# Stacked loads over two DMA queues, weight loads moved, and unread products in TensorE's waits, in a one-core decoder layer

## What is computed

```python
q, k = l2norm(q), l2norm(k)                       # self-attention
attn = softmax(einsum('bhnd,bhkd->bhnk', q/sqrt(D), k/sqrt(D)) / temperature)
x = layernorm(x + proj(attn @ v) + proj_b)
Srel = skew(einsum('bhsd,ld->bhsl', q, Er))       # cross-attention
attn = softmax(where(causal, (q @ k.T + Srel) / sqrt(dh), -inf))
x = layernorm(x + attn @ v)
top1 = argmax(softmax(x @ router_w + router_b))   # experts
for i in range(8):
    a, g = split(x @ w1[i] + b1[i])
    out += where(top1 == i, (a * sigmoid(g)) @ w2[i] + b2[i], 0)
x = layernorm(x + out)
```

## Time and profile before

| | us |
|---|---|
| median of 3 runs | 289.67 (287.71 to 290.94) |
| profiled execution, whole | 290.45 |
| its span, first to last instruction | 288.7 |
| TensorE busy in it | 235.4 |
| VectorE busy | 202.0 |
| ScalarE busy | 140.7 |
| GpSimd busy | 91.8 |
| mean granted clock of TensorE | 0.915 |

### The profile page before, as it was taken

One profiled execution on the slowest core, in us unless ns is written; L12 is line 12 of the kernel. 1 busy time (PEld: TensorE's weight loads), 2 busy tenths in 40 slices (PEclk: granted clock), 3 DMA queues, 4 the chain that ended last, 5 costly groups with the idle time before them and its releaser, 6 DMA issues.

```text
span 288.7 us, 8043 instructions
## 1 busy us (share of the span) xinstructions
PE 235.4 (82%) x3170; PEld 173.4 (60%) x3171; DVE 202.0 (70%) x579; ACT 140.7 (49%) x326; POOL 91.8 (32%) x128
## 2 busy tenths in 40 slices
...
PEclk9959799955999988999799899999999689999995
...
GB/s 65 195 396 184 41 168 154 109 76 179 218 60 166 104 119 22 94 189 213 94 111 112 3 41 70 190 115 115 194 175 61 16 20 187 187 179 345 141 7 0
DMA packets 30036, 36.92 MB, mean 128 GB/s; under 512 B 6967, under 2 KB 23333, under 8 KB 29616
## 3 DMA queue, kind: packets, MB, share of 16 engines
...
q10 hardware_dynamic: 256, 0.03, 0.1%
HBM read 25.00 MB, written 11.80 MB: 127 GB/s over the span
## 4 chain that ended last, share of the span: by engine, by line
PE 33%; issue 20%; DVE 17%; POOL 10%; DMA 9%; ACT 7%; SPq 2%; POOLq 1%; DVEq 0%; ACTq 0%
DVE negm L1084 6%; POOL out L777 5%; PE SB L1529 4%; PE MA L1365 3%; DMA w_sb<-parts_a 3%; POOL rs L772 3%; PE SA L1409 3%; DMA shift_a<-nmT 2%; DMA parts_a<-SpA 2%; PE MB L1345 2%; PE SA L1424 2%; PE SB L1388 2%; PE MA L1435 2%; ACT P L851 2%; SPq L467 2%
## 5 line engine op out<-in xcount | busy, mean ns | idle before, releaser
L1084 DVE TENSOR_REDUCE negm<-SA 128x2 bf16<-128x512 f32 x64 | 41.2, 685 | 11.4 <-PE SA L1409 11.0
L851 ACT ACTIVATE P<-SA 128x512 f32<-128x512 f32 x64 | 35.7, 599 | 14.6 <-PE SA L1424 13.1
L1163 DVE TENSOR_REDUCE negm<-MB 128x4 bf16<-128x512 bf16 x32 | 22.0, 686 | 8.3 <-PE MB L1345 8.0
L735 POOL TENSOR_TENSOR rs<-ve,half 128x2 f32<-128x2 f32 (+1 forms) x9 | 6.1, 682 | 64.9 <-DVE ve L1045 64.9
L797 ACT ACTIVATE Sb<-SB 128x512 bf16<-128x512 f32 x22 | 13.1, 597 | 24.5 <-PE SB L1529 24.2
L889 ACT ACTIVATE P2b<-SB 128x1024 f32<-128x1024 f32 x14 | 14.1, 1023 | 8.9 <-PE SB L1548 8.8
L1409 PE MATMUL SA<-w_sb 96*128 96x256 bf16 x64 | 12.5, 297 | 6.7 <-DVE negm L1084 4.7
L1524 PE MATMUL SB<-QH,KZ 128*128 128x64 bf16 x320 | 16.9, 198 | 1.1 <-DMA QH<-parts_b 1.1
L1435 PE MATMUL MA<-P,V 128*32 128x256 f32 x256 | 17.3, 402 | 0.0
L1548 PE MATMUL SB<-identb,negm 128*128 128x128 bf16 x176 | 14.3, 219 | 3.0 <-issue 1.9
L777 POOL DMA_INDIRECT out<-P,token x15 | 15.3, 1019 | 3.8 <-issue 3.1
...
## 6 DMA issues: line engine op xcount, KB each, us to landing
...
```

The lines of the kernel that those rows point to most:

```text
L851: a.activation(P1[:, grp % 2, kt, 2 * i:2 * i + 2, :].rearrange("p h t -> p (h t)"), SA[:, bank_a("st", b, u), :], ACT.Exp).then_inc(s["ex ...
L1084: v.tensor_reduce(out=negm1[:, hp // 4, qt, :, hp % 4], in_=SA[:, bank_a("d", b, u), :].rearrange("p (g k) -> p g k", g=2), axis=AX.X, op= ...
L1163: v.tensor_reduce(out=negm2[:, qb, :], in_=MBb[:, 0:512].rearrange("p (c k) -> p c k", c=4), axis=AX.X, op=ALU.max, negate=True).then_inc( ...
```

## The change

It has three parts. First, of the four stacked loads of a stage the two of the high rows (QS and KS rows 48 to 95, Z/QZ and QH from row 64) are issued by GpSimd instead of SP, with semaphores of their own (qs_high, qz_high, qh_high). For stage A GpSimd does this at A1.qsin; for stage B at a new step A2.zin, which stands some steps behind A2.q2T in batches 0 and 1 and right behind it in 2 and 3. A1.qsin.1 moves ahead of A1.k0.1. GpSimd waits there for the same writes as SP does. Second, W.u3 moves from behind B.tr3.1 to behind A2.ln1.2, W.pk0 from behind A2.k2T.2 to behind A2.zin.2, and W.u4 from behind B.sh2.1 to behind B.sc1.2. Third, TensorE gets steps K.w, each with a number of unread products (`unread`), at 18 places from batch 0's first transposes to the second batch's weighing, 46 products, and 2 more between the two products of A1.qkv.1. In batch 0's steps they write to MB, in batch 1's to bank 3 of SB.

```diff
-    A1.qkv.0 A1.vcp.0 A1.k1.1 A1.qkn.0 W.bl0.0 W.bl1.0 W.bl2.0 W.bl3.0 A1.qkT.0 A1.k5.0 A1.k2.0 A1.qkv.1 A1.ex0.0
...
-    A2.st4.0 A2.st5.0 A1.k6.0 A1.k0.1 A2.st6.0 A2.st7.0 A1.qsin.1 A2.pv0.0 A2.pv1.0 A2.st8.0 A2.st9.0 A2.k2T.0
-    A2.st11.2 A2.st12.2 B.tr3.1 W.u3.0 A2.k2T.2 W.pk0.0 A2.st13.2 B.sh2.1 W.u4.0 A2.st14.2 B.sh3.1 A2.st15.2 B.tr4.1
...
+    A1.qkv.0 A1.vcp.0 A1.k1.1 A1.qkn.0 W.bl0.0 W.bl1.0 W.bl2.0 W.bl3.0 K.w4.0 A1.qkT.0 A1.k5.0 A1.k2.0 K.w3.0
+    A1.qkv.1 A1.ex0.0 A1.ex1.0 A1.d0.0 A1.d1.0 A1.ex2.0 A1.ex3.0 A2.cx.0 A1.d2.0 A1.d3.0 A2.xpb.0 K.w2.0 A1.d4.0
+    A1.ex7.0 A1.d12.0 A1.d13.0 W.v6.0 K.w1.0 A1.d14.0 A1.d15.0 K.w3.0 A1.shT1.0 A1.qkn.1 A1.k8.1 A2.st0.0 A1.k4.0
+    A2.st1.0 A1.qkT.1 A2.st2.0 A2.st3.0 K.w1.0 A2.st4.0 A2.st5.0 A1.k6.0 A1.qsin.1 A1.k0.1 A2.st6.0 A2.st7.0
+    A2.pv0.0 A2.pv1.0 A2.st8.0 A2.st9.0 K.w1.0 A2.k2T.0 A2.st10.0 A2.st11.0 K.w3.0 A2.nm0.0 A2.st12.0 A1.k3.1
+    A2.st13.0 K.w2.0 A2.st14.0 W.u0.0 A2.st15.0 A2.pv2.0 A2.pv3.0 A1.d0.1 A1.d1.1 K.w2.0 A1.d2.1 A1.d3.1 A2.nm1.0
+    A1.d4.1 A1.vcp.1 A1.d5.1 A2.oT.0 A1.d6.1 A2.proj.0 A1.d7.1 A2.ln1.0 B.v.0 A1.qkv.2 K.w3.1 A1.shT0.1 A1.shin0.1
+    K.w2.1 A2.x1T.0 A1.d8.1 A1.d9.1 K.w2.1 A1.d10.1 A1.d11.1 A2.q2T.0 A1.d12.1 A1.d13.1 K.w7.1 A1.d14.1 A1.d15.1
+    A1.qkn.2 A2.zin.0 K.w1.1 A2.st0.1 A2.st1.1 A1.shT1.1 K.w3.1 A1.qkT.2 A1.shin1.1 B.build.0 A2.st2.1 A2.st3.1
+    K.w1.1 A2.st4.1 A2.st5.1 A2.st6.1 A2.st7.1 B.rest.0 A2.pv0.1 A2.pv1.1 K.w5.1 A2.st8.1 A2.cx.1 B.sc0.0 A2.nm0.1
...
+    A1.d2.3 A2.proj.2 A2.ln1.2 W.u3.0 B.sc6.1 B.sh5.1 B.pv0.1 A1.d3.3 A1.d4.3 A2.x1T.2 B.nm0.1 A2.q2T.2 A2.zin.2
+    W.pk0.0 A1.d5.3 B.tr6.1 A1.d6.3 A1.vcp.3 B.sc7.1 A1.d7.3 B.tr7.1 A1.d8.3 B.sh6.1 A1.d9.3 B.sh7.1 A1.d10.3
+    B.sc0.2 B.sc1.2 W.u4.0 B.tr0.2 A2.st0.3 B.sc2.2 A2.st1.3 B.tr1.2 A2.st2.3 B.sc3.2 B.tr2.2 B.sh0.2 B.sh1.2
...
-PACED_BY = {("A1", "qsin"): ("qs_in", 64, 0, 0), ("A1", "d"): ("sa_full", 16, 1, 1), ("A1", "shT0"): ("m_in0", 16, 0, 16),
-            ("A1", "shT1"): ("m_in1", 16, 0, 16), ("A2", "st"): ("st_full", 16, 1, 1), ("A2", "q2T"): ("qz_in", 32, 0, 32),
+PACED_BY = {("A1", "qsin"): ("qs_in", 32, 0, 0), ("A1", "d"): ("sa_full", 16, 1, 1), ("A1", "shT0"): ("m_in0", 16, 0, 16),
+            ("A1", "shT1"): ("m_in1", 16, 0, 16), ("A2", "st"): ("st_full", 16, 1, 1), ("A2", "q2T"): ("qz_in", 16, 0, 16),
...
             def q_k_in(b):
...
-                for g in range(2):
-                    rows = slice(g * SR, (g + 1) * SR)
-                    load(QSs[b % 2][rows, :, :].rearrange("r (a g j) t -> r g a (j t)", g=2, a=2)[:, g, :, :],
-                         half_stack(parts_a, 0, g).rearrange("r (a j) t -> r a (j t)", a=2), "qs_in")
-                    load(KSs[b % 2][rows, :, :], half_stack(parts_a, 1, g), "qs_in")
+                load(*query_rows(b, 0), "qs_in")
+                load(*key_rows(b, 0), "qs_in")
...
             def cross_queries(b):
...
-                for half_ in (0, 64):
-                    load(Zs[b % 2][half_:half_ + SR, :, q], stack(parts_b, 0)[:, :, q], "qz_in")
+                load(*cross_rows(b, 0), "qz_in")
...
-                by_half(lambda at, heads: QHs[b % 2][at:at + SR, heads, q], parts_b, 0, q, "qh_in")
+                load(*cross_half(b, 0), "qh_in")
...
+            def high_stacks(b):
+                wait(pool, "st_full", (b - 1) * 16)
+                pool.wait_ge(s["pa_out"], b * 96)
+                for rows, parts in (query_rows(b, 1), key_rows(b, 1)):
+                    pool.dma_start(rows, parts).then_inc(s["qs_high"], 16)
+
+            def high_queries(b):
+                wait(pool, "sc_full", (b - 1) * NQB)
+                if b < 2:
+                    pool.wait_ge(s["z_fill" if b == 0 else "qz_fill"], 1)
+                    pool.wait_ge(s["kz_fill" if b == 0 else "qh_fill"], 1)
+                pool.wait_ge(s["pq_out"], b * 48 + 48)
+                for name, (rows, parts) in (("qz_high", cross_rows(b, 1)), ("qh_high", cross_half(b, 1))):
+                    pool.dma_start(rows, parts).then_inc(s[name], 16)
...
-            def stay_busy(n):
+            def stay_busy(n, room=SB[:, 3, :]):
                 for _ in range(n):
-                    mm(SB[:, 3, :], identb[:, :], identb[:, :].unsqueeze(1).broadcast_to([P, 4, P]), start=True, stop=True)
+                    mm(room, identb[:, :], identb[:, :].unsqueeze(1).broadcast_to([P, 4, P]), start=True, stop=True)
+            def unread(b, n):
+                stay_busy(n, MB[:, :] if b == 0 else SB[:, 3, :])
...
+                    elif b == 1 and i == 0:
+                        unread(0, 2)
```

More of the change, by code:

```diff
@@ L68 @@
-    A2.st10.0 A2.st11.0 A2.nm0.0 A2.st12.0 A1.k3.1 A2.st13.0 A2.st14.0 W.u0.0 A2.st15.0 A2.pv2.0 A2.pv3.0 A1.d0.1
-    A1.d1.1 A1.d2.1 A1.d3.1 A2.nm1.0 A1.d4.1 A1.vcp.1 A1.d5.1 A2.oT.0 A1.d6.1 A2.proj.0 A1.d7.1 A2.ln1.0 B.v.0
-    A1.qkv.2 A1.shT0.1 A1.shin0.1 A2.x1T.0 A1.d8.1 A1.d9.1 A1.d10.1 A1.d11.1 A2.q2T.0 A1.d12.1 A1.d13.1 A1.d14.1
-    A1.d15.1 A1.qkn.2 A2.st0.1 A2.st1.1 A1.shT1.1 A1.qkT.2 A1.shin1.1 B.build.0 A2.st2.1 A2.st3.1 A2.st4.1 A2.st5.1
-    A2.st6.1 A2.st7.1 B.rest.0 A2.pv0.1 A2.pv1.1 A2.st8.1 A2.cx.1 B.sc0.0 A2.nm0.1 A2.st9.1 A2.st10.1 B.tr0.0
@@ L73 @@
-    B.sc1.0 A2.st11.1 A2.st12.1 B.sc2.0 A1.qsin.2 B.tr1.0 A2.xpb.1 A2.st13.1 A2.st14.1 A2.k2T.1 A2.st15.1 B.sc3.0
-    B.tr2.0 B.sh0.0 A2.pv2.1 A2.pv3.1 B.sh1.0 A1.d0.2 B.tr3.0 A1.d1.2 W.u1.0 W.v7.0 A2.nm1.1 A1.d2.2 B.sc4.0 B.sh2.0
-    A2.oT.1 B.sh3.0 A1.d3.2 B.tr4.0 A2.proj.1 A2.ln1.1 B.sc5.0 B.pv0.0 A1.d4.2 A2.x1T.1 A1.d5.2 B.sh4.0 B.nm0.0
-    A2.q2T.1 A1.d6.2 A1.d7.2 B.tr5.0 A1.vcp.2 A1.qkv.3 B.sc6.0 B.sh5.0 A1.d8.2 A1.d9.2 B.tr6.0 A1.qkn.3 B.sc7.0
-    A1.d10.2 B.sh6.0 A1.shT0.2 A1.shin0.2 B.tr7.0 A1.d11.2 A1.d12.2 A2.xpb.2 B.sh7.0 A1.d13.2 A1.d14.2 B.build.1
@@ L78 @@
-    B.pv1.0 A1.d15.2 A2.st0.2 B.nm1.0 A2.st1.2 A2.st2.2 B.ln2.0 B.v.1 A2.st3.2 W.u2.0 A1.shT1.2 A1.shin1.2 B.sc0.1
-    B.rest.1 A2.st4.2 A2.st5.2 A2.pv0.2 A2.st6.2 B.x2T.0 A2.st7.2 B.sc1.1 A2.cx.2 B.lg.0 A2.pv1.2 B.tr0.1 B.sc2.1
-    B.tr1.1 A2.st8.2 A2.st9.2 B.sh0.1 B.rk.0 A1.qkT.3 B.sh1.1 B.sc3.1 B.tr2.1 A2.nm0.2 A2.st10.2 B.sc4.1 A1.qsin.3
-    A2.st11.2 A2.st12.2 B.tr3.1 W.u3.0 A2.k2T.2 W.pk0.0 A2.st13.2 B.sh2.1 W.u4.0 A2.st14.2 B.sh3.1 A2.st15.2 B.tr4.1
-    A2.pv2.2 B.sc5.1 A2.pv3.2 B.sh4.1 B.tr5.1 A2.nm1.2 A1.d0.3 A1.d1.3 A2.oT.2 A1.d2.3 A2.proj.2 A2.ln1.2 B.sc6.1
@@ new lines @@
+    A2.nm1.1 A1.d2.2 B.sc4.0 B.sh2.0 A2.oT.1 B.sh3.0 A1.d3.2 B.tr4.0 A2.proj.1 A2.ln1.1 B.sc5.0 B.pv0.0 A1.d4.2
+    A2.x1T.1 A1.d5.2 B.sh4.0 B.nm0.0 A2.q2T.1 A1.d6.2 A1.d7.2 B.tr5.0 A1.vcp.2 A1.qkv.3 B.sc6.0 B.sh5.0 A1.d8.2
+    A1.d9.2 B.tr6.0 A1.qkn.3 A2.zin.1 B.sc7.0 A1.d10.2 B.sh6.0 A1.shT0.2 A1.shin0.2 B.tr7.0 A1.d11.2 A1.d12.2
+    A2.xpb.2 B.sh7.0 A1.d13.2 A1.d14.2 B.build.1 B.pv1.0 A1.d15.2 A2.st0.2 B.nm1.0 A2.st1.2 A2.st2.2 B.ln2.0 B.v.1
+    A2.st3.2 W.u2.0 A1.shT1.2 A1.shin1.2 B.sc0.1 B.rest.1 A2.st4.2 A2.st5.2 A2.pv0.2 A2.st6.2 B.x2T.0 A2.st7.2
```

79 lines of the change are left out of this document (48 added, 31 removed).

## The result

The changed kernel takes 296.3 us (median of 4 runs, 295.2 to 297.0), the kernel before, timed beside it, 290.3; the ratio is 1.022 with a 95% interval of 1.017 to 1.027. Slower, outside the range of 281.2 to 287.8, and on the side to which the prediction gave 0.05.

A forecast was written before the change was run, and what follows sets the result against it. It took a chain mostly through TensorE, with half-clock stretches and DMA waits, to bound the kernel. Terms summed to -5.8 us from the 289.67 median, hence 283.9 us; own range 282.3 to 285.6, 8 in 10 281.2 to 287.8.

The forecast's parts named there:

- Term c2: At st8.1 and B.sc0.0: halves on two queues land sooner, by the 172 against 148 GB/s ratio; -1.2 us.
- the software queue is served last: Rival, chance 0.08: GpSimd's halves land 8.2 to 8.8 us after issue, d0.3 starts at 137.8; 292.5 us.
- At batch 1 TensorE's weighing ends with the loads anyway, and at batch 2 it doesn't wait for them: nothing.: Split loads at batches 1 and 2: landing sooner was booked as no gain there.
- Terms a and b: Full clock from 14.4 (batch 0's projection and stackings), -1.75 us, and from 31.4 (batch 1's transposed rows), -0.45 us.
- a gain moves on whole, but for the clock: After each gain: later steps are released by earlier ones, so it reaches the end; clock shifts, no sign, 1.5 us.
- The cost of the products (+0.3): The 48 unread products on TensorE: 0.23 us each at full clock, fitting the waits they stand in; +0.3 us.
- Term d: Ahead of d0.3: without W.u3 and the picks beside them, batch 3's parts and split finish sooner; -2.4 us.
- Term e: At B.sc0.2: QH's high half 1.1 us sooner, against picks slowing the masking of Z; -0.3 us.
- Shared engines: Rival, chance 0.18: the two queues share the engines, so landings don't move; 285.3 us.
- Halves side by side: Rival, chance 0.12: halves no longer take turns in one queue, so loads land much sooner; 281.8 us.
- The clock is lost again later: Rival, chance 0.17: the clock isn't held or is lost later, and products at half clock overrun waits; 287.3 us.

The follow-up runs named there:

- e1: The changed kernel with all stacked loads issued by SyncE again, products and moved weight loads kept; 289.8 us against 289.2 before.
- e12: The changed kernel with only the high halves of Z, QZ and QH back on SyncE's queue; 287.1 us against 289.5 before.
- e2: The kernel before with the high halves on GpSimd's queue alone, no unread products, weight loads in old places; 294.3 us against 289.2 before.
- e3: The kernel before with the 48 unread products alone; 289.9 us against 289.2 before.
- e13: The changed kernel without the 26 late unread products, the front's 22 kept; 290.7 us against 288.8 before.
- e16: The kernel before with the front's 22 unread products alone; 289.8 us against 288.8 before.
- e8: The kernel before with the 48 unread products and 37 more in nine later waits of batches 1 to 3; 291.9 us against 289.4 before.
- e11: The changed kernel with all stacked loads on SyncE and only the front's 22 products, weight loads moved; 286.2 us against 289.5 before.
- e5: The kernel before with the split alone, sides swapped so GpSimd issues the low halves; 294.7 us against 289.4 before.
- e4: The kernel before with W.u3, W.pk0 and W.u4 at their new places alone; 288.3 us against 289.2 before.
- e6: The kernel before with only the high halves of QS and KS on GpSimd's queue; 292.7 us against 289.4 before.
- e7: The kernel before with only the high halves of Z, QZ and QH on GpSimd's queue; 294.6 us against 289.4 before.
- e18: The changed kernel timed again; 294.2 us against 289.9 before.
- e17: The e11 kernel timed again in more rounds; 288.3 us against 289.9 before.
- e15: The kernel before with the 26 late unread products alone; 290.6 us against 288.8 before.

## Why the prediction was wrong

- **Term c2, the halves on GpSimd's queue (-1.2, bounds 0 and -2.5): the step that failed, and in sign.** The bounds had no loss in them. The premise was that two queues move more, 172 GB/s against 148. But batch 0's own loads, all on SyncE's queue, had 171, and the change gave them 163. In place of landings 1.1 us sooner, Z's second half came 8.5 us after the first issue instead of 7.2, and the last of the four after 9.4 instead of 9.0. With the split taken out of the change (e1) its 6.0 us over before become 0.6, with stage B's alone taken out (e12) -2.3. By itself the split costs 5.1 us (e2), 1.15 of it at the end and, in the profiled execution, 1.8 behind a root that GpSimd computes late, for which the sum had 0.2; the change itself has 0.3 there. The sum should have gone by the landings of 8.2 and 8.8 us, which I gave to a rival at 0.08. That rival, *the software queue is served last*, had the lateness right and its places only in part: at batch 1 the high halves land 1.6 and 1.0 us after the low ones, under its 2.2, and d0.1 lost nothing; at batch 3 1.4 and 3.0, just at its 3, and d0.3 starts at 139.5 where it had 137.8. It missed the end of the program.
- **"At batch 1 TensorE's weighing ends with the loads anyway, and at batch 2 it doesn't wait for them: nothing."** So it was for QS and KS. But QZ and QH of batch 1 had no term in the sum at all: they land 9.6 us after the first issue instead of 8.9, the write of batch 2's shifts behind them, and TensorE waits 3.65 us. Most of that wait is not the split's: e1 has 2.60 and e3 3.00 without it, e13 0.58 with it and without the late products.
- **Terms a and b (-1.75, -0.45): right in their place, wrong as an account of the whole.** d0.1 came 2.9 us sooner in the change and 3.0 in e3. But "a gain moves on whole, but for the clock" is the second step that failed: e3 and e16 end where before does. Two things in the runs go with that. The next transfers are a wall: what comes sooner to the shifts waits longer for them (3.47 us in e1, 3.00 in e3 ahead of st0.2). And the half-clock stretches move; I gave them 1.5 us of no sign. Within the kernel before, the ten executions with a mean clock of 0.945 or more take 286.1 us, the 31 with less than 0.915 take 290.2: time and clock go together over 4 us, without that showing which sets the other. Between kernels they do not (e8 0.971 and 291.9, e11 0.935 and 286.2). The first stretch is itself not fixed: e2 and e5, without any unread product, have d0.0 at 17.6 and full clock from 14.4, while e4, e6 and e7 have 19.2 as before does. So in some executions term a is there without the products.
- **The cost of the products (+0.3): the third step that failed.** I priced their length and not what follows when TensorE comes sooner to a wait that a transfer ends. Each against its own before, the 26 late ones cost 4.1 us by the change against e13 (6.0 less 1.9; 2.4 by e18), 3.9 by e1 against e11 (2.1 by e17), 1.8 by themselves (e15). That they cost, and that they come with the longer waits ahead of st8.1 and st0.2, is shown. That the half clock behind these waits is how they cost is seen in the rows of four kernels but not separated: e3, e8 and e15 have the same products and full clock from 72 to 80.
- **Term d (-2.4): both halves of it right, and eaten.** The write of batch 3's parts ends 5.1 us after the first issue instead of 7.3 (127.15 to 132.26), the split is undisturbed. But the loads behind it take 7.1 us instead of 5.3, GpSimd's last 5.9 us after its issue. e4, without the split, starts d0.3 at 133.2, 3.1 sooner than before. At the end 0.9 of it is left, which its interval does not tell from nothing.
- **Term e (-0.3).** QH came later, not sooner. The masking beside GpSimd's copies took 1.19 us instead of 0.69. The last write of batch 3's shifts took 3.38 us in the change instead of 1.31, and not by W.u4, which had landed 0.1 us after its issue: in e4 W.u4 was in flight beside that write, which took 1.41, and in e3, with W.u4 in its old place, it took 3.31. Its cause is open.
- **The rivals.** *Shared engines* is nearly true of the last landing (9.1 us in e7, 9.4 in the change, 9.0 before) and says nothing on the order. *Halves side by side* fell. *The clock is lost again later* was right in that new half-clock stretches came; what they cost was not separated.

Taken by single parts, 5.1 (e2) + 0.7 (e3) - 0.9 (e4) = 4.9 us over before, where the change has 6.0 and, again, 4.3 (e18). That this comes out is in part luck, since other sums of parts do not: e6 and e7 make 8.4 for e2's 5.1, and e12, by e6, e3 and e4 3.0 over before, is 2.3 under it. Taking the split out of the change gives back 5.4 us, taking the late products out 4.1, so neither alone is the loss. What stays open is the part of e2's and e7's medians that their profiled executions do not show; and why e12 lies 8.3 us lower beside its before than the change for one stage's loads.
